# Feed-forward of a routed-expert kernel: both row transposes moved from TensorE to VectorE, one of them by way of DRAM

## The reference, cut to what matters

```python
x = x + attention(ctx, ctx, layernorm(x), ssm_kernel, D)      # not touched
h = layernorm(x).reshape(-1, 1024)
top_k_index, tkw = router(h)                                  # 8 of 32 experts for each token
xs = jnp.repeat(h, 8, axis=0)[argsort(top_k_index.reshape(-1))]
gate = jax.lax.ragged_dot(xs, w_gate, group_sizes)            # 1024 -> 512, one matrix an expert
up = jax.lax.ragged_dot(xs, w_up, group_sizes)
down = jax.lax.ragged_dot(silu(gate) * up, w_down, group_sizes)   # 512 -> 1024
routed = (down[unsort].reshape(T, 8, 1024) * tkw[..., None]).sum(axis=1)
shared = silu(h @ sw_gate) * (h @ sw_up) @ sw_down            # inner width 1024
x = x + routed + shared
```

## Time and profile before

| | |
|---|---|
| median of 3 runs | 14783.38 us (14782.56 to 14791.44) |
| the profiled execution's own time | 14714.25 us |
| its span, first to last instruction | 14712.6 us |
| TensorE busy | 14193.2 us, 96% of the span |
| VectorE, ScalarE, GpSimd busy | 36%, 21%, 29% |
| mean granted TensorE clock | 0.982 of full speed |
| DMA queues, share of 16 engines: GpSimd's q0, SyncE's q1, ScalarE's q10 | 18.1%, 14.2%, 1.1% |

### The profile page before, as it was taken

One profiled execution on the slowest core, in us unless ns is written; L12 is line 12 of the kernel. 1 busy time (PEld: TensorE's weight loads), 2 busy tenths in 40 slices (PEclk: granted clock), 3 DMA queues, 4 the chain that ended last, 5 costly groups with the idle time before them and its releaser, 6 DMA issues.

```text
span 14712.6 us, 197919 instructions
## 1 busy us (share of the span) xinstructions
PE 14193.2 (96%) x67488; PEld 11780.0 (80%) x67489; DVE 5244.6 (36%) x5698; ACT 3087.9 (21%) x4072; POOL 4249.8 (29%) x4357
## 2 busy tenths in 40 slices
PE   9888887799999999999999999999999999999999
PEld 7777776588888888888888888888888888888887
DVE  6776776212212222122212222223112112445454
ACT  4333332111111122112112122212111111111111
POOL 6677776211111111111111111111111112333333
PEclk9998998899999999999999999999999999999999
DMA  4555454312212232122212233223112112665666
GB/s 123 97 96 96 96 103 80 74 60 74 75 60 74 76 108 91 60 75 91 76 58 92 76 107 106 105 76 121 57 60 76 57 60 89 205 209 201 208 205 201
DMA packets 482745, 1491.07 MB, mean 101 GB/s; under 512 B 87745, under 2 KB 87873, under 8 KB 482450
## 3 DMA queue, kind: packets, MB, share of 16 engines
q0 software_dynamic: 286720, 890.00, 18.1%
q1 hardware_dynamic: 177938, 531.68, 14.2%
q10 hardware_dynamic: 17920, 67.12, 1.1%
HBM read 1083.97 MB, written 421.38 MB: 102 GB/s over the span
## 4 chain that ended last, share of the span: by engine, by line
PE 81%; DMA 0%; DVE 0%; issue 0%; ACT 0%; DVEq 0%; ACTq 0%; SPq 0%; POOLq 0%; POOL 0%
PE gps L1256 25%; PE ups L1256 25%; PE yps L1256 25%; PE xps L1263 4%; PE hps L1296 2%; DVE wlo L1184 0%; DMA raw<-in_L_ffn_w_up_dram 0%; ACT whi L1122 0%; DMA picked<-yd,gidx 0%; DMA xg<-xnd,idx 0%; DVE yrow L1210 0%; ACTq L1004 0%; DVEq L1004 0%; DVE xlo L1184 0%; DVE hlo L1184 0%
## 5 line engine op out<-in xcount | busy, mean ns | idle before, releaser
L1101 POOL DMA_INDIRECT yd<-yrow,yidx x544 | 576.3, 1059 | 7815.8 <-DVE yrow L1234 7815.8
L1220 DVE TENSOR_TENSOR hb<-hb,ups 128x512 f32<-128x512 f32 x672 | 461.9, 687 | 6191.7 <-ACT hb L1141 6191.7
L1256 PE MATMUL gps<-whi,xhi 128*128 128x512 f32 x5376 | 2160.2, 402 | 33.5 <-DVE wlo L1184 29.9
L1256 PE MATMUL gps<-whi,xlo 128*128 128x512 f32 x5376 | 2113.1, 393 | 0.0
L1256 PE MATMUL ups<-whi,xhi 128*128 128x512 f32 x5376 | 2113.0, 393 | 0.0
L1256 PE MATMUL ups<-whi,xlo 128*128 128x512 f32 x5376 | 2108.2, 392 | 0.0
L1256 PE MATMUL gps<-wlo,xhi 128*128 128x512 f32 x5376 | 2106.1, 392 | 0.0
L1256 PE MATMUL ups<-wlo,xhi 128*128 128x512 f32 x5376 | 2097.4, 390 | 0.0
L1141 ACT ACTIVATE hb<-gps 128x512 f32<-128x512 f32 x672 | 402.8, 599 | 6725.0 <-PE ups L1256 6714.7
L1256 PE MATMUL yps<-whi,hhi 128*128 128x512 f32 x5376 | 1724.5, 402 | 4.5 <-DVE hlo L1184 4.5
L1256 PE MATMUL yps<-wlo,hhi 128*128 128x512 f32 x5376 | 1674.9, 393 | 0.0
(11 more groups left out here) (166 smaller groups left out, 18095.4 us busy)
## 6 DMA issues: line engine op xcount, KB each, us to landing
raw<-in_L_ffn_w_gate_dram SPq DMA_DIRECT2D x128, 512.0 KB, 5.8
raw<-in_L_ffn_w_up_dram SPq DMA_DIRECT2D x128, 512.0 KB, 7.0
raw<-in_L_ffn_w_down_dram SPq DMA_DIRECT2D x64, 1024.0 KB, 7.0
kT<-in_ctx_dram SPq DMA_DIRECT2D x64, 704.0 KB, 15.6
xin<-in_x_dram SPq DMA_DIRECT2D x64, 512.0 KB
thi<-kph SPq DMA_DIRECT2D x64, 512.0 KB, 10.8
tlo<-kpl SPq DMA_DIRECT2D x64, 512.0 KB, 14.0
xres<-in_x_dram SPq DMA_DIRECT2D x64, 512.0 KB
```

The costliest lines, as they stand in the source:

```text
L1101: pool.indirect_dma_start(out=yd, in_=yrow[i][:, :], in_offset=None, out_offset=bass.IndirectOffsetOnAxis(ap=yidx[i][:, 0:1], axis=0), bou ...
L1220: dve.tensor_tensor(hb[:, :], hb[:, :], ups[:, :], ALU.mult).then_inc(h_done, 1)
L1256: ins = pe.matmul(ps, rows, w[:, chunk, i * 512:(i + 1) * 512], start=first and n == 0, stop=last_one and n == 2)
```

## The change

- **Token rows.** The gather of 128 rows of 1024 becomes four gathers (`xg[:, q, :]`) of quarter rows of 256, from a view of `xnd` with four entries for each token. Partition 32b+s gets quarter b of four tokens. `x_turn` on VectorE then does one `transpose`, which turns blocks of 32x32, into the PSUM tensor `xt`. `xhi` and `xlo` are made from `xt`. The list holds four times the token number, is loaded with its 32x4 entries repeated for four groups of partitions, and GpSimd adds the group's number (`xidx`). TensorE's 8 transposes go.
- **Gated rows.** VectorE writes silu(gate)*up to PSUM (`hp`), waits for it, and transposes the 32x32 blocks back to `hb`. ScalarE's queue issues four stores of 64 KB to DRAM (`spread_h`), waits for all of them, and issues one load of 256 KB to `hz` (`collect_h`); `hhi` and `hlo` are made from `hz`. TensorE's 4 transposes go.
- **Weights** lie in DRAM in the order of rows that the blocks ask for, gate beside up: one load of 1 MB for each pair of chunks in place of two of 512 KB.
- **Order of the queues.** ScalarE and VectorE take `xhi` and `xlo` of t+1 ahead of silu and the product of t. `spread_h` stands behind `split_gu` on ScalarE. `x_turn` of tile t+2 stands behind `split_gu` on VectorE. In a tile with sums, `yps` is added first and the four picks last, behind `hlo`. GpSimd takes the list and the gathers of rows ahead of the picks. There are four pick buffers, as before.
- **Stores of sums** are issued by SyncE, each ahead of the fetch that reuses its buffer.
- **Constants** are loaded again in `plan` and no longer kept.

```diff
             def gather(t, slot, turns):
 
-                wait(pool, xT_mm, t - 1 if not isinstance(t, int) else max(t - 1, 0))
+                wait(pool, x_turned, t - 1 if not isinstance(t, int) else max(t - 1, 0))
                 pool.wait_ge(idx_ld[slot], 16 * (turns + 1))
...
+                pool.tensor_tensor(xidx[slot][:, :], idx[slot][:, :], quad[:, :], ALU.add).then_inc(xidx_ready, 1)
+                pool.wait_ge(xidx_ready, t + 1)
+                for q in range(QUADS):
+                    settle(pool, pool_turns)
+                    pool.indirect_dma_start(out=xg[slot][:, q, :], out_offset=None, in_=quarters,
+                                            in_offset=bass.IndirectOffsetOnAxis(ap=xidx[slot][:, q:q + 1], axis=0))\
+                        .then_inc(x_ld[slot], 16)
...
             def x_high(t):
-                act.wait_ge(xT_mm, t + 1)
-                act.activation(xhi[:, :, :].rearrange("p k t -> p (k t)"), xps[:, :], ACT.Copy).then_inc(x_hi, 1)
+                act.wait_ge(x_turned, t + 1)
+                wait(act, gu_mm, t)
+                act.activation(xhi[:, :, :], xt[:, :, :], ACT.Copy).then_inc(x_hi, 1)
+
+            def spread_h(t, slot):
+
+                act.wait_ge(h_turned, t + 1)
+                for q in range(QUADS):
+                    act.dma_start(hsd[slot].rearrange("(b r) q x -> r b q x", r=SQ)[:, :, q, :],
+                                  hb[q * SQ:(q + 1) * SQ, :].rearrange("r (b x) -> r b x", x=P)).then_inc(h_st, 16)
+
+            def collect_h(t, slot):
+                act.wait_ge(h_st, 16 * QUADS * (t + 1))
+                wait(act, h_lo, t)
+                act.dma_start(hz[:, :, :, :].rearrange("p q k s -> p (q k s)"),
+                              hsd[slot].rearrange("p q x -> p (q x)")).then_inc(h_ld, 16)
 
             def tile(c):
                 t = c.n()
-                store_sum(c)
+                if c.on(1):
+                    x_high(c.n(1))
                 if c.on():
                     act.wait_ge(gu_mm, t + 1)
-                    wait(act, hT_mm, t)
+                    wait(act, h_st, 16 * QUADS * t)
                     act.activation(hb[:, :], gps[:, :], ACT.Silu).then_inc(silu_done, 1)
                 if c.on(1):
-                    x_high(c.n(1))
                     if c.part(-1) != 1:
                         with act.If(entry(act, c.n(1), F_FIRST, 1) == 1):
                             split_gu(entry(act, c.n(1), F_EXPERT, NE - 1))
+                if c.on():
+                    spread_h(t, c.slot())
...
                 if c.on():
-                    act.wait_ge(hT_mm, t + 1)
...
+                    collect_h(t, c.slot())
+                    act.wait_ge(h_ld, 16 * (t + 1))
+                    wait(act, down_mm, t)
+                    act.activation(hhi[:, :, :].rearrange("p k (q s) -> p q k s", s=SQ), hz[:, :, :, :], ACT.Copy)\
+                        .then_inc(h_hi, 1)
...
+            def x_turn(t, slot, turns):
+
+                dve.wait_ge(x_ld[slot], 16 * QUADS * (turns + 1))
+                wait(dve, x_lo, t)
+                dve.transpose(xt[:, :, :].rearrange("p k t -> p (k t)"),
+                              xg[slot][:, :, :].rearrange("p q (k r) -> p k q r", r=SQ)).then_inc(x_turned, 1)
+
...
             def tile(c):
                 t = c.n()
+                if c.on(1):
+                    x_low(c.n(1))
                 if c.on():
                     dve.wait_ge(silu_done, t + 1)
-                    dve.tensor_tensor(hb[:, :], hb[:, :], ups[:, :], ALU.mult).then_inc(h_done, 1)
+                    dve.tensor_tensor(hp[:, :], hb[:, :], ups[:, :], ALU.mult).then_inc(h_done, 1)
+                    dve.wait_ge(h_done, t + 1)
+                    dve.transpose(hb[:, :], hp[:, :]).then_inc(h_turned, 1)
                 if c.on(1):
-                    x_low(c.n(1))
                     if c.part(-1) != 1:
                         with dve.If(entry(dve, c.n(1), F_FIRST, 1) == 1):
                             split_gu(entry(dve, c.n(1), F_EXPERT, NE - 1))
+                if c.on(2):
+                    x_turn(c.n(2), c.slot(2), c.half(2))
                 i = c.slot(-1)
                 if c.part(-1) is not None:
-                    add_picks(c.n(-1 - SH0), i, c.half(-1 - SH0), c.part(-1))
+                    dve.wait_ge(acc_ld[i], 16 * (c.half(-1 - SH0) + 1))
                     dve.wait_ge(down_mm, t)
                     dve.tensor_tensor(yrow[i][:, :], yrow[i][:, :], yps[:, :], ALU.add).then_inc(y_dve, 1)
...
+                if c.part(-1) is not None:
+                    dve.wait_ge(y_dve, t)
+                    add_picks(c.n(-1 - SH0), i, c.half(-1 - SH0), c.part(-1))
...
+            x_turn(0, 0, 0)
             split_gu(0)
             x_low(0)
+            x_turn(1, 1, 0)
...
-                if c.on(1):
-                    transpose_rows(c.n(1), c.slot(1), c.half(1))
...
-                if c.on():
-                    pe.wait_ge(h_done, t + 1)
-                    for m in range(KH):
-                        last = pe.transpose(hps[:, m * P:(m + 1) * P], hb[:, m * P:(m + 1) * P], ident)
-                    last.then_inc(hT_mm, 1)
```

More of the change, by code:

```diff
@@ L197, in expert_weights @@
     one = slice(e, e + 1) if isinstance(e, int) else bass.ds(e, 1)
-    return [A[k][one].rearrange("o a b -> (o a) b") for k in ("w_gate", "w_up", "w_down")]
+    return [A[k][one].rearrange("o p k i -> (o p) k i") for k in ("w_gu", "w_dn")]
 def head_rows(t, head):
@@ L1010, in _, with before_unit, wait_for @@
         def _(sp):
-            def load(e, weights):
-                def before_unit(q):
+            def before_unit(e):
+                def wait_for(q):
                     if q < GU:
@@ L1017, in before_unit @@
                         sp.wait_ge(lo_dn, DN * (e - 1) + q - GU + 1)
[L1018 to L1025, removed]
+                return wait_for
+            with sp.Fori(1, NE) as e:
+                load_weights(sp, raw, w_ld, *expert_weights(A, e), before_unit(e))
             sp.wait_ge(y_st[0], 16 * SH0 // 2)
@@ L1176, in _ @@
             walk_tiles(act, tile)
-            store_sum(Tile(TILES + 1))
-            for i in range(2):
-                act.wait_ge(out_st[i], 16 * NTILE // 2)
         @block.vector
@@ L1236, in tile @@
                     dve.wait_ge(h_hi, t + 1)
-                    low(hlo[:, :, :].rearrange("p k t -> p (k t)"), hps[:, :],
-                        hhi[:, :, :].rearrange("p k t -> p (k t)")).then_inc(h_lo, 1)
+                    low(hlo[:, :, :].rearrange("p k (q s) -> p q k s", s=SQ), hz[:, :, :, :],
+                        hhi[:, :, :].rearrange("p k (q s) -> p q k s", s=SQ)).then_inc(h_lo, 1)
                 if c.fixed and t == 0:
@@ L1243, in tile @@
                         split_dn(entry(dve, t, F_EXPERT, NE - 1))
+                if c.part(-1) is not None:
+                    dve.wait_ge(y_dve, t)
+                    add_picks(c.n(-1 - SH0), i, c.half(-1 - SH0), c.part(-1))
+            for q in range(QUADS):
+                last = dve.tensor_copy(quad[:, q:q + 1], quarter[:, :])
+            last.then_inc(quad_ready, 1)
+            x_turn(0, 0, 0)
             split_gu(0)
             x_low(0)
+            x_turn(1, 1, 0)
             walk_tiles(dve, tile)
@@ L1258, in three @@
                 return ins
-            def transpose_rows(t, slot, turns):
-                pe.wait_ge(x_ld[slot], 16 * (turns + 1))
-                for m in range(KX):
-                    last = pe.transpose(xps[:, m * P:(m + 1) * P], xg[slot][:, m * P:(m + 1) * P], ident)
-                last.then_inc(xT_mm, 1)
             def tile(c):
@@ L1330, in program, with blocks_of_rows, weights @@
         feed_forward(nc, A, keep)
-_INS = ["x", "ctx", "L0_xattn_ssm_kernel", "L0_xattn_D", "L0_ffn_router_w", "L0_ffn_router_bias",
-        "L0_ffn_w_gate", "L0_ffn_w_up", "L0_ffn_w_down", "L0_ffn_sw_gate", "L0_ffn_sw_up", "L0_ffn_sw_down"]
+_INS = ["x", "ctx", "L0_xattn_ssm_kernel", "L0_xattn_D", "L0_ffn_router_w", "L0_ffn_router_bias"]
+def blocks_of_rows(w, chunks):
+    e, _, n = w.shape
+    return w.reshape(e, QUADS, chunks, SQ, n).transpose(0, 1, 3, 2, 4).reshape(e, P, chunks, n)
+def weights(gate, up, down, sw_gate, sw_up, sw_down):
+    import numpy as np
+    parts = [slice(s * I, (s + 1) * I) for s in range(NE - E)]
+    gate = np.concatenate([gate] + [sw_gate[None, :, c] for c in parts])
+    up = np.concatenate([up] + [sw_up[None, :, c] for c in parts])
+    down = np.concatenate([down] + [sw_down[None, c, :] for c in parts])
+    return blocks_of_rows(np.concatenate([gate, up], axis=2), KX), blocks_of_rows(down, KH)
 def keys(ctx):
```

137 lines of the change are left out of this document (75 added, 62 removed).

## The result

The changed kernel takes 14833.11 us, median of 7 runs (14826.86 to 14837.36), the one before 14782.56 us (14774.14 to 14792.29). The ratio is 1.0034, 95% interval 1.0022 to 1.0045: slower by 0.34% where 3.1% faster was forecast. The profiled execution's span is 14829.8 us.

The account below looks back on a forecast made before the run. TensorE, busy 96% of the span, was taken as the bound. Terms -880 + 132 + 265 + 18 = -465 us against 14714 gave 14249 us profiled, predicted as 14320 us timed, 3.1% faster; range 13930 to 14800 us.

Parts of the forecast that it names:

- part 5: Tiles with sums: period is 9.8 us plus L, or 16.51 if longer; 18.6 us a tile, +265 us in 127 tiles.
- L: Round trip of h through DRAM, issues and landings of stores and load: 8.3 us in routed tiles, 8.8 with sums.
- the ring decides: Rival, tiles with sums: VectorE's passes, picks and L set the period; slower beyond 22.3 us a tile, 15160 us; chance 0.16.
- The term of +265 us: Tiles with sums: 2.09 us a tile over 16.51 us, in 127 tiles.
- Part 1: TensorE: its transposes leave, freeing 1.31 us in each of 672 tiles, -880 us; period 16.51 us.
- Part 2: Way of x: VectorE turns take 1.23 us (x) and 0.69 us (h); four GpSimd gathers stay hidden from TensorE.
- Part 3: Way of h in a routed tile: `hlo` ends 13.6 us after gate and up, needed at 16.5; hidden, 2.9 us cover.
- Part 4: Changes of expert: two covers lost, `yps` waits for `hlo`; 4 us a change, 33 changes, +132 us.
- Part 6: Ends of the kernel: first matmul 12 us later, last round trip and picks +6 us; together +18 us.
- Hidden everywhere: Rival, tiles with sums: L at most 6.7 us, so the +265 goes; -730, 14050 us; chance 0.22.
- GpSimd becomes the limit: Rival, tiles with sums: VectorE holds up GpSimd's indirect DMAs, 21.2 us a tile, 14650 us; chance 0.08.

Follow-up runs that it names:

- The experiments on L: Changed kernel with picks' gathers cut to 64 of 1024 columns: 0.9851 of before; separately, with SyncE's sum store held until the next tile's `hhi`: 0.9883.
- the run with the old distance: Changed kernel with its three small index tensors allocated behind `hlo`, so `xhi` lies 106688 bytes behind `whi` as before: 0.9924 of before.
- The version without the trip: Changed kernel with token rows still turned on VectorE but gated rows again by TensorE's transposes, no DRAM trip: 14441.5 us, 0.9747 of before.
- the second profile of before: Kernel before, no edit, profiled once more: 14808.31 us; last list write of the router issued at 2735.65 us.
- the early picks: Changed kernel with the four picks added right after `yps`, ahead of `hlo`: 14320.77 us, 0.9667 of before.

## Why the prediction was wrong

**The step that failed is part 5, the size of L.** The mechanism was right, period = passes + L, and also that the kernel gets slower if the ring decides. The term of +265 us measured 589: (20.43 - 16.51) x 63 + (21.86 - 16.51) x 64. L was 10.0 and 12.1 us, not 8.8. Its pieces, as medians from start to start:

| stretch, us | forecast for the sums | routed | sums, first half | second half |
|---|---|---|---|---|
| first to last issue of the stores, with hand-offs | 1.3 | 1.3 | 1.6 | 3.9 |
| last of these to the load's issue | 4.0 | 1.9 | 5.5 | 5.4 |
| from there to `hhi` | 3.5 | 2.6 | 2.8 | 2.8 |

So the load was priced high and the stores too low. I had argued that the picks "should have mostly landed" when the stores of h go out. By the landings of before they can't have:

```profile
13041.82 0.94 POOL L1110 DMA_INDIRECT picked<-yd,gidx  x1 [0.30 <-issue]
```

```profile
13043.97 2.17 ACTq L1173 DMA_DIRECT2D hsd<-hb  x4
```

The last gather is 2.2 us old when the first store of h is issued, and in the trace of before the picks' gathers took 4.1 us or more to land, 6.1 in the median. The sum's store is 3.1 us old (issued at 13040.87), and such a store took 6.7 us. The experiments on L show that both count. VectorE's part was 10.4 us in the first half and not 9.8, from gaps of 0.4 to 1.1 us that the trace marks as issue; in the second half it was 9.8. My rival "the ring decides" had its point at 22.3 us a tile; 21.1 on average was enough, because of the next item.

**A term was missing: the rate of the matmuls.** I wrote that what is left is the same matmuls. They were, at the same granted clock, but 1.6% slower, 16.80 in place of 16.51 us a tile. That is 0.29 x 544 = 158 us in the routed tiles (in the sums TensorE wasn't the bound), and the run with the old distance gave 162 back. 324 + 158 of the 515 us between the forecast of -465 and the measured +50.5 are these two. The rate alone doesn't explain the miss: with the old distance the kernel still took 0.9924 of before, where 0.969 was forecast.

**Part 1** held: 1.31 us a tile left TensorE, and no `xps` or `hps` remains.

**Part 2** held: 1.26 and 0.72 us for the turns against 1.23 and 0.69, and four gathers a tile stayed hidden in ordinary tiles, which took TensorE's own 16.80 us.

**Part 3** held in that the trip is hidden, with L at 5.9 us and not 8.3. The Trainium skill, page "DMA: Bandwidth & Descriptors", section "Anatomy of one DMA", whose figure is for the software path, gave the estimate of 6.05 us; routed tiles agree with it on ScalarE's queue, and the stage with sums was 4 to 6 us above it.

**Part 4** came to the right size by the wrong way, and that was luck. Forecast 132 us; the routed stage lost 158 us beyond its period (9269.0 - 540 x 16.80 = 197, less 39 in before). At an ordinary change the tile is 1.7 us longer (median), not 4, and `yps` waited for `hlo` once, for 0.8 us, since `spread_h` is not held up by the split. ScalarE at a change:

```profile
3350.22 3.72 ACT L1155 ACTIVATE whi<-raw 128x2048 fp32r<-128x2048 f32 x2
3352.37 1.78 ACTq L1173 DMA_DIRECT2D hsd<-hb  x4
3353.84 1.90 ACT L1155 ACTIVATE whi<-raw 128x2048 fp32r<-128x2048 f32 x1
3355.57 0.35 ACTq L1179 DMA_DIRECT2D hz<-hsd  x1
3355.64 1.91 ACT L1155 ACTIVATE whi<-raw 128x2048 fp32r<-128x2048 f32 x1
```

The stores stand behind all four pieces of the split in the program and are issued during the second; even the load goes out before the last piece starts. Changes of this kind make 34 tiles longer, by 67 us together.

The rest lies in ten tiles of 11 to 15 us more, 129 us together, where before had three (37 us). All ten stand where an expert with a single tile makes two changes follow each other. One of the seven that before doesn't have is shown below, from SyncE's queue, the chain, ScalarE and TensorE. `split_dn` stands on ScalarE behind `hhi`, and `hhi` came late: the last store of h was issued while SyncE issued six weight loads of 1 MB, and landed after 14.4 us.

```profile
5206.48 2.52 SPq L197 DMA_DIRECT2D raw<-in_w_dn_dram  x2
5209.65 2.81 SPq L194 DMA_DIRECT2D raw<-in_w_gu_dram  x4
```

```profile
5212.41 14.41 DMA hsd<-hb
```

```profile
5230.19 0.63 ACT L1204 ACTIVATE hhi<-hz 128x512 fp32r<-128x512 f32 x1 [16.60 <-DMA hz<-hsd]
```

```profile
5235.89 1.22 PE L1311 MATMUL yps<-whi,hhi 128*128 128x512 f32 x2 [12.41 <-DVE wlo L1221]
```

Over the routed tiles from 3000 to 11000 us TensorE's waits for the low parts of new weights sum to (us, times, longest):

```profile
PE yps L1311 <- DVE wlo L1221: 90.6, 10, 13.0
PE gps L1311 <- DVE wlo L1221: 74.5, 31, 12.5
```

The version without the trip has three such tiles, the same three as before, and lost some 55 us beyond its period of 17.23 us in the routed stage. So the trip is what makes the other seven. I had looked at one change only, and not at how close they come.

**Part 6**: +9 (or nothing against the second profile of before) and +20 in place of +12 and +6. At the end nothing covers the last trip, and TensorE's `yps` waited up to 13.9 us for `hlo`.

**The rivals.** "Hidden everywhere" is excluded by the result itself, 20.4 and 21.9 us a tile with sums, and "GpSimd becomes the limit" by the early picks. "The ring decides and the kernel gets slower" came true, at 0.16, at the short end of what I had given it.

## What to carry to other kernels

When work is put behind a wait "last in the tile", ask what the next tile needs from that engine: a latency that was free for the matmuls becomes part of a ring with everything queued behind it, and moving the long pass in front of the wait gave back 3.7% here. Price a transfer by landings at the moment of its own issue, beside the stores and gathers that are released by the same event, and check the stretches where the rare cases follow each other. And compare the mean of the unchanged instructions first: 96 bytes of index tensors, allocated between weights and rows, cost 1.1% here.

## What the runs showed that was not expected

- How far the rows lie behind the weights in SBUF changes the rate of the fp32r matmuls of 128x512: with `xhi` 106688 bytes behind `whi` 24 of them took 5.49 to 5.51 us, with 106720, 106784 and 106816 bytes 5.59 to 5.60 us, at the same granted clock. Moving both by 32 bytes changed nothing.
- ScalarE issues DMAs while earlier activations of its queue are still to run: the stores queued behind four activations (7.3 us in all) went out 2.2 us after the first of them began.
- Four issues of a 64 KB store took 1.8 us on ScalarE's queue in routed tiles and 5.0 us in the second half of the sums, but 1.8 us there too once the picks came early.
- The stage ahead of the one studied ended 89 us apart in two executions of the same program (2646.61 and 2735.65 us).
